# Softmax attention with a routed feed-forward layer: maxima two pairs ahead, weighing in one piece, low parts on GpSimd

## The reference, cut to what matters

```python
q = (layernorm(x) @ w_q.T + b_q) * 32 ** -0.5;  k = ctx @ w_k.T + b_k;  v = ctx @ w_v.T + b_v
scores = einsum("bthd,bshd->bhts", q, k) + bias[None]      # bias [1, 224, 750]
scores = where(mask[b, s], -3.4e38, scores)
x = x + (softmax(scores) @ v).reshape(B, T, E) @ w_o.T + b_o
y = layernorm(x)                                           # then: distances of y to 32 prototypes,
x = x + sum_over_2_nearest(weight * (A[i] @ (B[i] @ y) + bias[i]))
```

## Time and profile before

| what | value |
|---|---|
| the profiled execution | 936.89 us, span 935.1 us |
| mean granted TensorE clock | 0.974 |
| TensorE matmuls busy | 871.4 us, 93% of the span |
| VectorE busy | 748.0 us, 80% |
| GpSimd busy | 517.7 us, 55% |
| ScalarE busy | 475.7 us, 51% |

### The profile page before, as it was taken

One profiled execution on the slowest core, in us unless ns is written; L12 is line 12 of the kernel. 1 busy time (PEld: TensorE's weight loads), 2 busy tenths in 40 slices (PEclk: granted clock), 3 DMA queues, 4 the chain that ended last, 5 costly groups with the idle time before them and its releaser, 6 DMA issues. The chain is left out here.

```text
span 935.1 us, 17178 instructions
## 1 busy us (share of the span) xinstructions
PE 871.4 (93%) x6328; PEld 651.5 (70%) x6328; DVE 748.0 (80%) x1539; ACT 475.7 (51%) x985; POOL 517.7 (55%) x550
## 2 busy tenths in 40 slices
PE   6969999999999999999999999999989989699998
PEld 6857767776777677667766776777645557588986
DVE  5568898889888888888898889888867766787774
ACT  5325555555555555555555655555534432445653
POOL 4058576667767675766586667667863324340000
PEclk9979999999999999999999999999959999799999
DMA  8775555565466556655554555455666303110111
GB/s 283 228 172 131 146 136 125 141 157 136 117 166 151 141 129 164 154 147 140 148 137 120 136 154 149 104 148 138 162 172 148 87 30 110 41 61 30 31 31 49
DMA packets 81237, 120.41 MB, mean 129 GB/s; under 512 B 8565, under 2 KB 60587, under 8 KB 81154
## 3 DMA queue, kind: packets, MB, share of 16 engines
q1 hardware_dynamic: 79089, 112.27, 47.2%
q0 software_dynamic: 2064, 7.05, 2.6%
HBM read 80.00 MB, written 39.28 MB: 128 GB/s over the span
## 5 line engine op out<-in xcount | busy, mean ns | idle before, releaser
L667 ACT ACTIVATE probs_sb<-probs_sb,neg_keep 125x448 f32<-125x448 f32 x384 | 245.6, 664 | 280.0 <-DVE probs_sb L850 279.3
L839 DVE CUSTOM_DVE_ANT_0 biased<-score_ps,neg_bias 112x750 f32<-112x750 f32 x256 | 238.7, 932 | 29.1 <-PE score_ps L1055 27.1
L850 DVE TENSOR_TENSOR probs_sb<-st_ps,neg_bias_t 125x448 f32<-125x448 f32 x384 | 226.3, 617 | 29.5 <-PE st_ps L1076 29.3
L534 POOL TENSOR_TENSOR sums_two<-probs_sb 125x448 f32<-125x448 f32 x112 | 128.9, 1151 | 172.2 <-ACT probs_sb L667 108.7
L1055 PE MATMUL score_ps<-k_st,q_st 98*112 98x512 f32 (+1 forms) x512 | 143.7, 362 | 24.2 <-DVE neg_max L839 17.6
L1076 PEld LDWEIGHTS st_ps<-q_st,k_st 98*125 98x125 f32 x768 | 114.8, 191 | 56.9 <-DVE probs_sb L850 28.0
L1076 PE MATMUL st_ps<-q_st,k_st 98*125 98x224 f32 x768 | 137.6, 288 | 15.1 <-DVE probs_sb L850 10.6
L536 POOL TENSOR_TENSOR sums_two<-sums_two,probs_sb 125x448 f32<-125x448 f32 x112 | 129.3, 1154 | 8.8
L1055 PEld LDWEIGHTS score_ps<-k_st,q_st 98*112 98x112 f32 x512 | 79.1, 180 | 74.6 <-issue 35.4
L998 PE MATMUL acc<-ctx_hi,w_hi 128*128 128x376 f32 (+1 forms) x256 | 89.4, 349 | 7.4 <-DVE ctx_lo L880 6.7
L998 PE MATMUL acc<-ctx_lo,w_hi 128*128 128x376 f32 (+1 forms) x256 | 89.5, 350 | 0.0
(11 more groups left out here) (204 smaller groups left out, 1669.9 us busy)
## 6 DMA issues: line engine op xcount, KB each, us to landing
k_st<-k_parts SPq DMA_DIRECT2D x96, 375.0 KB
k_parts<-kq_parts SPq DMA_DIRECT2D x60, 188.0 KB, 5.9
k_parts<-kq_parts SPq DMA_DIRECT2D x60, 187.0 KB, 6.0
q_st<-q_parts SPq DMA_DIRECT2D x96, 112.0 KB
ctx_raw<-in_ctx_t SPq DMA_DIRECT2D x14, 752.0 KB, 5.9
q_parts<-kq_parts SPq DMA_DIRECT2D x30, 224.0 KB, 3.8
xb<-in_x SPq DMA_DIRECT2D x8, 448.0 KB, 8.3
attn_t<-attn SPq DMA_DIRECT2D x32, 112.0 KB, 1.9
```

The costliest lines, as they stand in the source:

```text
L534: eng.tensor_tensor(sums_two[:, :], tile[0], tile[1], ALU.add).then_inc(two_ready, 1)
L667: nc.scalar.activation(probs_sb[0:SW, at:at + 2, :], probs_sb[0:SW, at:at + 2, :], ACT.Exp, scale=neg_keep[:, q // PB:q // PB + 1]).then_i ...
L839: nc.vector.tensor_tensor_reduce(out=biased[:, :], in0=score_ps[:, 0:S], in1=neg_bias[:, w % TC, :], scale=1.0, scalar=FMAX, op0=ALU.add, ...
L850: nc.vector.tensor_tensor(probs_sb[0:SW, at:at + 2, :], st_ps[(BANKS * q + j) % 2][0:SW, 0:2 * T].rearrange("p (s t) -> p s t", s=2), neg_ ...
```

## The change

- **Maxima two pairs ahead.** TensorE's `score` and `turn_max`, VectorE's `add` and ScalarE's `round_max` and `max_row` serve pair `q + 2` (the first score piece `q + 3`) in the step of pair `q`. `turned_score(q + 1, 0)` is issued at the end of step `q`. The prologue does one more pair.
- **Staged keys by half groups.** `load_keys(n, half)` brings two heads; there are twice as many DMAs of half the size. The first half of group `n + 2` is issued at `h == 3`, the second half of `n + 1` at `h == 1`. `load_x(1)` moves behind the first key loads.
- **Weighing and sums.** `weigh` is one piece of 24 products, `sum_up` one piece of 24 products with `ones`; `sum_tiles` on GpSimd goes away. VectorE's `output` is cut into `invert` (`h == 2`, last of the step) and `output` (`h == 3`).
- **Low parts.** ScalarE copies a key or query tile in full (`copy_tile`) and so frees `acc`; GpSimd makes `hi` and `lo` from the copy (`split_tile`). VectorE's `low_tile` is left only for batch 0. The normalisation of `x` moves from VectorE to ScalarE.
- **Shares.** `h == 1` pairs get a quarter share of projection steps, `PIECES` and the positions of the query tiles and of `X_AT` are other ones.
- **`finish`.** The parts of the expert bias (`bst`) are made behind the first routing on VectorE, small loads have semaphores of their own, and `distances(1)` stands ahead of the loop on TensorE.

```diff
-PIECES = (0.17, 0.28, 0.56, 0.77, 0.88)
+PIECES = (0.1, 0.28, 0.45, 0.6, 0.72)
+SUM_SHARE = 0.25
...
+            def split_tile(b, n):                          # GpSimd
...
+                    eng.wait_ge(k_copied, tile_copied(NT * b + n)[1])
+                    eng.wait_ge(k_stored[r], 32 * before)
+                    eng.tensor_scalar(k_hi[r][:, 0:SH[f]], k_full[r][:, 0:SH[f]], 1.0, 0.0, ALU.mult, ALU.add)\
+                       .then_inc(part_hi_done, 1)
+                    eng.wait_ge(part_hi_done, parts)
+                    eng.tensor_tensor(k_lo[r][:, 0:SH[f]], k_full[r][:, 0:SH[f]], k_hi[r][:, 0:SH[f]].bitcast(F32),
+                                      ALU.subtract).then_inc(k_ready, 1)
...
+            def sum_up(n):                                 # TensorE
+                for s, h in itertools.product(range(ST), range(HG)):
+                    last = nc.tensor.matmul(out_ps[h * D:(h + 1) * D, 256:256 + T], ones[0:SW, :],
+                                            probs_sb[0:SW, (HG * n + h) % SLOTS * ST + s, :],
+                                            start=(s == 0), stop=(s == ST - 1))
+                last.then_inc(weigh_done, 1)
...
                 beside(0)                                  # TensorE, the step of pair q
                 if q < PAIRS:
-                    turned_score(q, 0)
                     turned_score(q, 1)
                 beside(1)
-                if q + 1 < PAIRS:
-                    score(TC * (q + 1) + 1)
+                if q + 2 < PAIRS:
+                    score(TC * (q + 2) + 1)
                 beside(2)
                 if q < PAIRS:
                     turned_score(q, 2)
...
                 beside(3)
-                if q + 2 < PAIRS:
-                    score(TC * (q + 2))
+                if q + 1 < PAIRS:
+                    turned_score(q + 1, 0)
+                if h == 1 and n:
+                    weigh(n - 1)
+                if q + 3 < PAIRS:
+                    score(TC * (q + 3))
                 beside(4)
...
-                if q + 1 < PAIRS:
-                    turn_max(q + 1)
+                if q + 2 < PAIRS:
+                    turn_max(q + 2)
+                if h == 1 and n:
+                    sum_up(n - 1)
                 beside(5)
```

More of the change, by code:

```diff
@@ L108 @@
 WEIGHT = {KEYS: 171, VALUES: 231, QUERIES: 110}
-X_AT = (2, 3)
+X_AT = (3, 4)
 def tiles_of(b):
@@ L130, in step_shares @@
     cost = [WEIGHT[kind] for kind, i in tiles_of(b) for m in range(STEPS[kind])]
-    share = sum(cost) / len([u for u in range(PB) if u % HG != 1])
+    weight = [SUM_SHARE if u % HG == 1 else 1.0 for u in range(PB)]
     cuts, at, given, spent = [], 0, 0.0, 0.0
     for u in range(PB):
-        given += share if u % HG != 1 else 0.0
+        given += weight[u] / sum(weight) * sum(cost)
         start = at
@@ L163, in ended, with keys_loaded, tile_copied @@
     return [(b, n) for n in range(NT) for p in pieces if cuts[p] < ends[n] <= cuts[p + 1]]
-def keys_loaded(n):
+def keys_loaded(n, half):
     return sum(96 + (16 if m % NG < 2 else 0) + (16 if m >= 2 else 0) for m in range(n % 2, n + 1, 2))
+def tile_copied(pos):
+    kind, count = tile_count(pos)
+    return kind, count - [k for k, i in FIRST_TILES].count(kind)
 class Shared:
@@ L341, in weave @@
         q_stored = [sem(f"q_stored{r}") for r in range(2)]
-        kq_loaded = [sem(f"kq_loaded{p}") for p in range(2)]
+        kq_loaded = [[sem(f"kq_loaded{p}_{half}") for half in range(2)] for p in range(2)]
         score_ready = sem("score_ready")
@@ L609, in _ @@
                     add_output_bias(eng, sh, bo_row, sh.xr_loaded, i + 1)
+                for tile in ended(q, 0, 1, 2, 3, 4, 5):
+                    split_tile(*tile)
             root(B)
@@ L893, in _ @@
                     keep_signs()
-                    add(0)
-                    add(1)
+                    for w in range(2 * TC):
+                        add(w)
                 low_tile(0, n)
@@ L962, in _ @@
                     normalise_rows()
+                if q == 0:
+                    for c in range(TC):
+                        x_stats(1, c)
+                    x_variance(1)
+                if q == 2:
+                    newton(1)
+                    negate_mean(1)
                 if b < B - 2:
@@ L1109, in spread_masked @@
+            def sum_up(n):
+                for s, h in itertools.product(range(ST), range(HG)):
+                    last = nc.tensor.matmul(out_ps[h * D:(h + 1) * D, 256:256 + T], ones[0:SW, :],
+                                            probs_sb[0:SW, (HG * n + h) % SLOTS * ST + s, :],
+                                            start=(s == 0), stop=(s == ST - 1))
+                last.then_inc(weigh_done, 1)
             def spread_masked():
```

324 lines of the change are left out of this document (184 added, 140 removed).

## The result

The changed kernel takes 940.6 us (median of seven runs, 939.8 to 941.5), the kernel before, timed beside it, 936.0 us. The ratio is 1.0041, its 95% interval 1.0027 to 1.0056: **slower by 0.4%**, where 915.0 us and "faster" were forecast, and outside the range of 899 to 933. The profiled execution spans 938.0 us, against 935.1.

What follows compares the result with a forecast made beforehand. The steady state was taken as TensorE's work plus 1.5 to 1.9 us of waits on VectorE a group. 936.9 - 8 (steady groups) - 9 (last batch) - 1 (start) - 3 (`finish`) = 915.9, against the median 915.0; range 899 to 933.

Steps and rivals of the forecast that it cites:

- The work is 20.1 us ... 1.5 to 1.9 us of waits in each group: Steady state, TensorE: 20.1 us of work in a head group; the remainder of 21.6 to 22.05 us is waits on VectorE.
- TensorE loses 0.7 us: Weighing and sums, each in one piece on TensorE, cost 5.2 us a group against 4.5 before.
- I take 0.9 us of waits: TensorE's waits in a steady group after the change: 0.9 us, with bounds 0 and 1.9.
- VectorE's low parts: Steady state: VectorE loses low parts, query tiles and normalisations, about 8 us a batch, 2 a group.
- The gaps of VectorE at a weighing, 3.6 us: VectorE stands about 1.9 us behind the weighing and 1.7 us behind the sums in each group, and can afford it.
- loads come late: Rival: twice the load issues make loads late by 1 us in each of 30 groups; 945 us, chance 0.04.
- the weighing block becomes a wait: Rival: VectorE idles 3.6 us while TensorE weighs, cannot catch up and hands the delay back; 947 us, chance 0.13.
- The edits at nothing: Steady state: the changed shares of GpSimd, SyncE (more load issues) and ScalarE (normalisation) were costed at nothing.
- The last batch, -9: Last batch: groups of 21.5 us gain 5 us, the last two reciprocals 4 to 5 more; 9 us, between 3 and 14.
- The start, -1: Start: first score near 51 us, but one more pair of maxima before the first turned score; gain 1, from -2 to 4.
- The last stage, -3: `finish`: bias parts moved behind VectorE's routing and `distances(1)` into the gap gain 3 us, between 0 and 5.

Runs made afterwards that it cites:

- Experiment 2: The kernel before with the sums of all batches on TensorE and none on GpSimd, nothing else changed: 976.5 us, ratio 1.044.
- Experiments 1 and 5: Both against the changed kernel: 1 left out five of six key tiles of the sums, 881.2 us; 5 cut weighing and sums into six pieces again, 973.4 us.
- experiment 3: The changed kernel with the low parts of keys and queries of batches 1 to 7 back on VectorE, sums still on TensorE: 992.5 us, ratio 1.061.
- experiment 7: The new order alone: sums of batches 0 to 6 on GpSimd, low parts on VectorE, weighing in six pieces as in the kernel before: 971.4 us, ratio 1.035.
- experiment 9: Two runs of the changed kernel: with the last stage of the kernel before, 939.5 us; with whole instead of half key loads, 938.5 us.
- b_two_blocks: The kernel before with the weighing in one piece at the fifth place of the step and the four sum products at the sixth: 1011.0 us, ratio 1.081.

## Why the prediction was wrong, step by step

- **"The work is 20.1 us ... 1.5 to 1.9 us of waits in each group": the step that failed.** The work was read from a few undisturbed intervals, and all that was left of 22.05 was called waits. The ledger gives 20.9 of work and 1.1 of waits for VectorE. What I missed is small: the turning of `x` (0.15 a group), and 0.7 in gaps between instructions that no row puts down to a wait. Experiment 2 bears it out from the other side: the kernel before took up 0.5 us of added work a group, not 1.5. The direct reading stood in the trace: TensorE's idle time for VectorE, 28.2 us in the whole run, 0.9 a group. So the waits, this step's term, were taken at nearly twice their size.
- **"TensorE loses 0.7 us": right.** By the ledger (instructions and rest) it went from 83.8 to 86.3 us a batch, 0.6 a group. Experiments 1 and 5 give its two halves, +1.9 for the sums and -1.1 to -1.3 for the pieces.
- **"I take 0.9 us of waits": right** (3.2/4 = 0.8 after). So the gain in waits was 0.3 a group, not 0.7 to 1.0, and the 0.6 to 0.7 of work stood against it: +9.3 us, where -8 was forecast. That is 17.3 of the 25.6 us by which the time was missed.
- **VectorE's low parts: the gain in waits was sized by VectorE's 2 us a group and its spare time.** Taken alone the move is worth 52 us in the new order (experiment 3); VectorE also stood before each for ScalarE. But the new order had lost 35 (experiment 7), and this loss I had at nothing: I had held the order to be what shortens waits. In the ledger the order raised the waits of a batch from 4.4 to 7.0 us, and the low parts' move took them from 8.2 to 3.2. That what was left of them came near the forecast (0.8 a group, for 0.9) is luck.
- **The gaps of VectorE at a weighing, 3.6 us: right.** 2.2 + 1.75 measured, and VectorE could afford them. The rivals "loads come late", 945, and "the weighing block becomes a wait", 947, were nearest in time, yet neither mechanism occurred: no load was late, and in the steady part the waits fell.
- **The edits at nothing: right** for GpSimd, SyncE and ScalarE; loads are never late (experiment 9).
- **The last batch, -9: measured -7.3, in part by luck.** The groups took 21.1 us each (760.21 - 675.94 over 4), where 21.5 was forecast. The windows show a cause that I had not counted on in full: before, the granted clock was low from 678 to 688 and from 691 to 702 us, 10 us lost by 1 less the clock; after, from 686 to 690 and from 700 to 707, 5 us lost. So up to 5 of the 7.3 us are the clock (an estimate). The last two reciprocals are 11.66 us apart, where 10 to 11 was forecast, but 2.3 of it is only that the reciprocal before comes late. Their sums lie 14.0 apart, for 15.4 before, so 1.4 us were gained and not 4 to 5. TensorE waits there for VectorE and ScalarE (1.85 and 0.81 us), and the weighing behind them takes 3.58 us at a mean clock of 0.62.
- **The start, -1: +0.1.** The first score came at 50.19 us (forecast 51), and the first turned piece at 57.08, for 62.28 before: 5.2 us ahead, more than I had thought. Part of it is that the granted clock was 1.00 there and 0.64 in that stretch of before, which I did not foresee. Up to the sums of group 0 it was all lost again: TensorE stood 3.5 us for VectorE on the way there, 2.19 of them before one score, against 1.1 of standing before. What took the rest stays open.
- **The last stage, -3: +0.8.** The bias parts fell beside GpSimd's work on `at_lo` and `xb`, as the trace of after shows:

```profile
799.77 2.00 DVE L1524 CAST bst<-bst_hi 32x512 fp32r<-32x512 f32 x1
801.79 1.65 DVE L1526 TENSOR_TENSOR bst<-bst_raw,bst_hi 32x512 fp32r<-32x512 f32 x1
803.45 1.39 DVE L1524 CAST bst<-bst_hi 32x512 fp32r<-32x512 f32 x1
804.86 0.69 DVE L1526 TENSOR_TENSOR bst<-bst_raw,bst_hi 32x512 fp32r<-32x512 f32 x1
```

```profile
799.41 2.08 POOL L230 TENSOR_TENSOR at_lo<-kq_parts,at_hi 128x896 fp32r<-128x896 f32 x1
801.46 3.11 POOL L237 TENSOR_TENSOR xb<-kq_parts,bo_row 112x512 f32<-112x512 f32 x2
```

```profile
805.60 1.75 PE L1772 MATMUL big<-ident,route_wide 112*128 112x112 f32 x8 [5.46 <-DVE bst L1526]
```

5.7 us for the four, where they took 3.4 before and 2.3 in the run with the old finish (0.41, 0.68, 0.54 and 0.69, with no operation of GpSimd beside them), and TensorE stood for the last of them. The first turned routes came 33.7 us behind the last reciprocal, for 33.3 before. The Trainium skill says that a copy of VectorE can hold the port pair shared with GpSimd, and that one of the two then waits for the other's whole instruction ("SBUF — State Buffer", "Who interferes with whom"); here the trace agrees, with copies of 2.00 and 1.39 us beside GpSimd against 0.41 and 0.54 without. I had worked out what the rule costs, 1 to 2.5 us, and kept the 3 in the sum.

## What to carry to other kernels

Read waits from the bottleneck engine's own idle time by releaser, over the whole run and by stage, before calling the remainder of a busy account "waits": the remainder holds all that the account forgot. Ask next how much added work those waits can take up: here none of it in the changed kernel (59.4 of 59 us came off), and a quarter in the kernel before (40.5 of 53 came on). A change of several parts can hide a good one behind a bad one: keeping the low parts on GpSimd and taking the sums of 20 of the 32 groups off TensorE again turned +0.4% into -2.3%.

## What the runs showed of the hardware that I had not expected

- A busy share says little of what an engine costs others: VectorE was at 72 and 73% in two runs 52 us apart. In the slower one it stood 34.9 us for ScalarE in front of the low parts, and TensorE's waits for VectorE went from 29.7 to 54.7 us.
- A short stand ahead of a block of small instructions went with a low clock in the block. In `b_two_blocks` TensorE stood 0.91 us and was busy 2.90 of the 4.00 us that include it; the granted clock was 0.50 in the first half of the weighing, which took 3.70 us. In the changed kernel it was busy 3.50 of the 4.00 us ahead of the same block, which ran at 1.00 in 2.41 us. These are two places of two kernels, and no run measured what decides:

```profile
260.90:264.90 4.00, 3.50 (x20) 2.53 (x18) 3.27 (x7) 3.04 (x6) 1.53 (x2) 1.00 0.41 109
264.90:267.31 2.41, 2.41 (x49) 1.46 (x49) 0.87 (x3) 1.08 (x3) 0.00 (x0) 1.00 0.63 170
```

- Six pieces instead of two blocks cost 5.0 us a batch (94.5 against 89.5), more than half of what all the added sums cost (7.6), though the instructions are the same.
